# Normalizing attention rows after they are replicated, and letting the next chunk's first two score matmuls go ahead of the scaling of the last

## What is computed

```python
x = x + _L0_attn_ref(_layernorm(x), ...)     # the change is in here
x = x + _L0_ffn_ref(_layernorm(x), ...)      # shared MLP and 8 experts
x = x + _L1_attn_ref(_layernorm(x), ...)     # two scans (Mamba), forward and backward
x = x + _L1_ffn_ref(_layernorm(x), ...)      # int8-rounded matmul

# in _L0_attn_ref, 16 heads of 64, Qc and Rc of 128
scores = jnp.einsum('bqhd,bkhd->bhqk', Qc, Rc)
norm = jnp.sqrt(jnp.sum(jnp.square(scores), axis=-1, keepdims=True))
attn = scores / jnp.maximum(norm, NORM_EPS)            # NORM_EPS = 1e-12
out = jnp.einsum('bhqk,bkhd->bqhd', attn, Hv).reshape(B, S, D_MODEL)
return out @ Wo + bo
```

## Time and profile before

| | |
|---|---|
| median of 2 runs | 9504.41 us (9500.37 and 9508.46) |
| profiled execution, time | 9552.86 us |
| profiled execution, span of the slowest core (core 2) | 9551.2 us |
| spans of the 8 cores | 9483.5 to 9551.2 us |
| PE busy | 4446.2 us (47%) |
| DVE busy | 4802.7 us (50%) |
| ACT busy | 3157.2 us (33%) |
| mean granted TensorE clock | 0.61 |

### The profile page before, as it was taken

How to read it: one execution, slowest core, us unless ns; L and a number is a source line. 1 busy time by engine, 2 the same in 40 slices (tenths; PEclk the granted TensorE clock), 3 DMA queues, 4 the chain that set the end, 5 groups by cost and what they waited for, 6 DMA issues and landing times.

```text
span 9551.2 us, 57267 instructions; the slowest of 8 cores (9483.5 to 9551.2 us)
## 1 busy us (share of the span) xinstructions
PE 4446.2 (47%) x11136; PEld 1264.4 (13%) x11136; DVE 4802.7 (50%) x8041; ACT 3157.2 (33%) x4385; POOL 172.2 (2%) x221
## 2 busy tenths in 40 slices
PE   3644555455556499996323232333323232323334
PEld 1211111111111133111000000000000000000112
DVE  2334343344334321224467675757576776767445
ACT  3333323332332121002243443434252534444321
POOL 0000000000000100000000000000000000000000
PEclk8766766666666687666555555555555555555556
DMA  1042572100000133110000000000000000000000
GB/s 45 6 36 23 69 83 25 16 2 4 4 0 0 16 122 110 53 53 9 10 3 16 5 16 7 12 10 10 14 7 16 4 17 3 16 7 13 25 12 36
DMA packets 203005, 222.92 MB, mean 23 GB/s; under 512 B 131441, under 2 KB 140049, under 8 KB 200561
## 3 DMA queue, kind: packets, MB, share of 16 engines
q0 software_dynamic: 141104, 76.50, 7.3%
q1 hardware_dynamic: 61570, 142.76, 4.6%
HBM read 278.07 MB, written 65.03 MB: 36 GB/s over the span
## 4 chain that ended last, share of the span: by engine, by line
DVE 40%; PE 32%; issue 12%; ACT 12%; DMA 2%; DVEq 1%; POOL 0%; ACTq 0%; SPq 0%; POOLq 0%
DVE HBF L1721 14%; PE P2U L200 10%; PE PSU L200 6%; DVE DBXP L1717 5%; PE PSU L848 3%; PE PSU L857 3%; PE P3U L200 3%; DVE SROW L817 2%; DVE XCC L1446 2%; DVE SCBW L876 1%; DVEq L35 1%; PE P3U L1773 1%; DVE CARRY L1726 1%; PE P4U L200 1%; ACT L1645 1%
## 5 line engine op out<-in xcount | busy, mean ns | idle before, releaser
L1693 PE MATMUL P3U<-DBXP,EYEB 128*128 128x512 bf16 x1024 | 576.3, 563 | 1974.7 <-DVE DBXP L1728 1974.1
L1721 DVE TENSOR_TENSOR_SCAN HBF<-DAP,CARRY,DBXP 128x512 bf16<-128x512 bf16 x1024 | 1314.6, 1284 | 109.6 <-DVE DBXP L1717 4.1
L876 DVE CAST SCBW<-PSU 128x512 bf16<-128x512 f32 x512 | 354.1, 692 | 774.8 <-PE PSU L848 770.7
L1717 DVE TENSOR_TENSOR DBXP<-U_CH,BREP 128x512 bf16<-128x512 bf16 x1024 | 429.5, 419 | 309.2 <-ACT DAP L1645 187.3
L857 PE MATMUL PSU<-SCBW,HV 128*64 128x512 bf16 x960 | 465.1, 484 | 153.8 <-DVE SCBW L876 118.5
L848 PE MATMUL PSU<-QCB,RCB 128*128 128x512 bf16 x1024 | 477.7, 476 | 66.5 <-DVE ATTO L894 53.4
L886 ACT CAST SCBW<-PSU 128x512 bf16<-128x512 f32 x512 | 300.1, 586 | 570.4 <-PE PSU L848 569.7
L200 PE MATMUL P2U<-YLN,W1E 128*128 128x512 bf16 x512 | 462.1, 1079 | 10.6 <-DMA W1E<-wfsc 10.6
L1657 ACT ACTIVATE DAP<-DT_CH,ACOL 128x512 bf16<-128x512 bf16 x512 | 359.0, 719 | 304.1 <-DVE HBF L1721 298.8
L1693 PEld LDWEIGHTS P3U<-DBXP,EYEB 128*128 128x128 bf16 x1024 | 106.7, 104 | 2450.1 <-issue 2449.7
L1728 DVE TENSOR_TENSOR DBXP<-HBF,CREP 128x512 bf16<-128x512 bf16 x1024 | 424.9, 415 | 1.9 <-issue 1.9
(11 more groups left out here) (324 smaller groups left out, 7457.3 us busy)
## 6 DMA issues: line engine op xcount, KB each, us to landing
wfsc<-L_ffn_w POOLq DMA_DIRECT2D x16, 2048.0 KB, 90.4
SW1H<-wfsc SPq DMA_DIRECT2D x64, 256.0 KB, 2.7
SW3H<-wfsc SPq DMA_DIRECT2D x64, 256.0 KB, 2.9
SW2C<-wfsc SPq DMA_DIRECT2D x32, 512.0 KB, 4.0
W1E<-wfsc SPq DMA_DIRECT2D x8, 2048.0 KB, 12.2
W2E<-wfsc SPq DMA_DIRECT2D x8, 2048.0 KB, 7.8
WINS<-wmsc SPq DMA_DIRECT2D x64, 256.0 KB, 2.6
WINZ<-wmsc SPq DMA_DIRECT2D x64, 256.0 KB, 2.6
```

The source lines that it names most:

```text
L876: b.sV.inc(v.tensor_copy(SCBW[kt % 2][:], PSU[kt % 2][:, :]))
L1693: b.sT.inc(t.matmul(ybank[:, :], EYEB[:], DBXP[ni % 2][:], start=(ni == 0), stop=(ni == 7)))
L1717: b.sV.inc(v.tensor_mul(DBXP[ni % 2][:], U_CH[:, dt * QC:(dt + 1) * QC], BREP[:, ni * QC:(ni + 1) * QC]))
L1721: b.sV.inc(v.tensor_tensor_scan(HBF[ni % 2][:], DAP[ni % 4][:], DBXP[ni % 2][:], CARRY[:, dt * 16 + n: dt * 16 + n + 1], ALU.mult, ALU.add))
```

## The change

Two things are changed in the code of one head.

Steps 2 and 3 change places. The squared norms are replicated first (rn_mm, rn_ev), and square root, maximum and reciprocal are then taken on the replicated tile RNREP, on 128 partitions, in four pieces of 128x512, each in place: `_rne_s` (ScalarE) issues four square roots, `_rne_v` (VectorE) waits for each and issues its maximum and its reciprocal. The instructions on the 1x2048 row are gone (one square root, one maximum, one reciprocal), and twelve come in.

In `_sc_t`, scores 0 and 1 of chunks 1 to 3 of a head wait for the counts taken behind the copies of the chunk before (prev_sc), which don't contain L894. For chunk 0 they wait as before, now for `_rne_v` too. The wait for vcur, which contains L894 of the chunk before, now stands ahead of the values matmul of tile 0, the first to write PSU2.

```diff
--- before.py
+++ after.py
@@ -805,31 +805,38 @@
                         return s.copy(ROW_A[0:1, i * QC:(i + 1) * QC], bank[0:1, :])
                     mm_evac(NQ, ns_mm, ns_ev, [PSU[0], PSU[1]], "s")
 
-                    def _rn_s(s):
-                        b.sS.wait(s)
-                        b.sS.inc(s.activation(ROW_B, ROW_A, AF.Sqrt))
-                    b.s(_rn_s)
-
-                    def _rn_v(v):
-                        b.sS.wait(v)
-                        b.sV.inc(v.tensor_scalar(ROW_B, ROW_B, C_TINY[0:1, :], None, ALU.max))
-                        b.sV.wait(v)
-                        b.sV.inc(v.reciprocal(ROW_A, ROW_B))
-                    b.v(_rn_v)
-
                     def rn_mm(t, i, bank):
-                        if i == 0:
-                            b.sV.wait(t)
                         return mm_group(t, bank[:, :],
                                         [(ONESF[:], ROW_A[0:1, i * QC:(i + 1) * QC])])
 
                     def rn_ev(s, i, bank):
                         return s.copy(RNREP[:, i * QC:(i + 1) * QC], bank[:, :])
                     mm_evac(NQ, rn_mm, rn_ev, [PSU[0], PSU[1]], "s")
-
+                    sb_rn = b.sS.n
+
+                    def _rne_s(s):
+                        for qc in range(NQ):
+                            b.sS.wait(s)
+                            b.sS.inc(s.activation(RNREP[:, qc * QC:(qc + 1) * QC],
+                                                  RNREP[:, qc * QC:(qc + 1) * QC], AF.Sqrt))
+                    b.s(_rne_s)
+
+                    def _rne_v(v, sb_rn=sb_rn):
+                        for qc in range(NQ):
+                            b.sS.wait(v, sb_rn + qc + 1)
+                            b.sV.inc(v.tensor_scalar(RNREP[:, qc * QC:(qc + 1) * QC],
+                                                     RNREP[:, qc * QC:(qc + 1) * QC],
+                                                     C_TINY, None, ALU.max))
+                            b.sV.wait(v)
+                            b.sV.inc(v.reciprocal(RNREP[:, qc * QC:(qc + 1) * QC],
+                                                  RNREP[:, qc * QC:(qc + 1) * QC]))
+                    b.v(_rne_v)
+
+                    prev_sc = None
                     for qc in range(NQ):
                         scm, avm, evm2 = {}, {}, {}
                         vcur, scur = b.sV.n, b.sS.n
+                        kt2_v, kt2_s = prev_sc if prev_sc else (vcur, scur)
                         for kt in range(16):
                             if kt % 2 == 0:
                                 evm2[kt] = (b.sV, vcur + kt // 2 + 1)
@@ -837,11 +844,11 @@
                                 evm2[kt] = (b.sS, scur + kt // 2 + 1)
 
                         def _sc_t(t, qc=qc, scm=scm, avm=avm, evm2=evm2, vcur=vcur,
-                                  scur=scur, qcb=qcb, rcb=rcb, hh=hh):
+                                  kt2_v=kt2_v, kt2_s=kt2_s, qcb=qcb, rcb=rcb, hh=hh):
                             for kt in range(16):
                                 if kt < 2:
-                                    b.sV.wait(t, vcur)
-                                    b.sS.wait(t, scur)
+                                    b.sV.wait(t, kt2_v)
+                                    b.sS.wait(t, kt2_s)
                                 else:
                                     sm, cnt = evm2[kt - 2]
                                     sm.wait(t, cnt)
@@ -852,6 +859,8 @@
                                 scm[kt] = b.sT.n
                                 if kt >= 1:
                                     k2 = kt - 1
+                                    if k2 == 0:
+                                        b.sV.wait(t, vcur)
                                     sm, cnt = evm2[k2]
                                     sm.wait(t, cnt)
                                     b.sT.inc(t.matmul(
@@ -885,6 +894,7 @@
                                     b.sT.wait(s, avm[kt - 2])
                                 b.sS.inc(s.copy(SCBW[kt % 2][:], PSU[kt % 2][:, :]))
                         b.s(_sc_s)
+                        prev_sc = (b.sV.n, b.sS.n)
                         if hh == 1 and qc == NQ - 1:
                             pair_free[hp].append((b.sS, b.sS.n))
```

## The result

| | before | after |
|---|---|---|
| median, us | 9515.23 (10 runs, 9494.17 to 9564.32) | 9417.13 (11 runs, 9391.40 to 9457.40) |
| ratio | | 0.989, 95% interval 0.9869 to 0.9912 |
| span of the slowest core in the profile | 9551.2 (core 2) | 9439.9 (core 3) |
| mean granted clock of the cores | 0.611 to 0.618 | 0.620 to 0.626 |

The changed kernel is 1.1% faster; 9419 us with a range of 9370 to 9460 was predicted. The new instructions are the square root L820, maximum L827 and reciprocal L831, and the copy out of the replicated row is L813.

The account below looks back on a forecast made before the run. Bound: heads run serially on every engine, with the norms row alone and passages stalled by L894, ACT's branch and clock falls. Passages -56, clock -36, norms +7 make -85 us, from median 9504.4 to 9419; range 9370 to 9460.

Parts of the forecast that it names:

- The waits at a passage: Between chunks, scores 0 and 1 no longer wait for L894: 1.17 us sooner at 48 passages, 56 us saved.
- everything behind ACT comes 1.17 us sooner: At a passage, ACT's table load starts at 1084.47 instead of 1085.64, and all behind ACT moves with it.
- The clock: Behind passages, half of the 48 clock falls go, 36 us saved; bounds 0 to 72 us.
- price for a fall: Behind a passage, 12 matmuls at 0.55 instead of 0.43 us each: 1.5 us per clock fall.
- rival 1: The clock falls at every passage as before: -56 + 7, 9455 us; chance 0.18.
- The norms: From last L805 copy to first score, 18.65 us against 18.20: 0.45 us worse per head, +7 us over 16.
- the maximum: In the norms, each of four DVE maxima on 128x512 takes 0.49 us.
- the seven gaps: In the norms, seven gaps of 0.10 us between dependent DVE instructions, 0.70 us per head.
- The reciprocal itself: In the norms, each of four 128x512 reciprocals on DVE takes 3.35 us.
- rival 3: DVE's branch ends last at a passage: only 0.63 us won each, 30 us, giving 9481 us; chance 0.08.
- rival 4: In the norms, the wide reciprocal is dearer, 8.10 us each: 304 us more, 9723 us; chance 0.03.
- The wait for weights (WHD): Weight loads, 18.3 us once before; PE beginning to wait for them in each head would show the forecast wrong.

Follow-up runs that it names:

- x3_fill_before: Kernel before plus unread matmuls in chunks 1 to 3, three ahead of score 0 and one ahead of the first values matmul; 9430.84 us, ratio 0.9919.
- x8_all: Changed kernel plus ones-matrix norm sums, reciprocals in pieces behind VectorE's copies, three unread matmuls per passage and early table load; 8942.45 us, ratio 0.9402.

## Why the prediction was right, point by point

- **The waits at a passage: right in size, slightly high in worth.** 1.17 us sooner at the second values matmul was forecast; 4.20 to 3.02 was measured, 1.18. What a passage gained by it at a steady clock is 15.68 - 14.59 = 1.09 us: 52 us for 56. That everything behind ACT comes 1.17 us sooner is the step that is slightly wrong, since DVE takes over. In passages that keep their clock (x3_fill_before for the waits of before), DVE's first copy starts 1.97 us behind the last values matmul before and 1.22 after, and its third at 5.75 and 4.64. Its copies come 1.71 apart at the high clock; only the third of before is 0.36 later than that, because score 4 stands behind the values matmul that waits for ACT. So ACT's branch held the old passage up by 0.36 us beyond DVE's, and the changed one is decided by DVE, as the early table load confirms.
- **The clock: right in kind, and the half was luck.** The prediction took half of the falls as gone, from a new passage that lay between two that it could see; it says itself that no row decides it. 170 of 384 were left, 44%, so 56% were gone. It also has both stops ahead of the fall, but by the earlier trace rows the clock fell between 1085.9 and 1086.1, inside the second stop (1085.56 to 1086.27). Its price for a fall, 1.5 us, was 1.47 by the inserted matmuls, but a fall in the changed kernel costs 1.24, with 4.8 us at 0.50 in place of 6.9, so 45 us were won for the 36 forecast. The rule of the Trainium skill ("TensorE: Matmul & The Clock Gate", A second HAM failure mode: psum-queue depth-cycling), that small standstills between groups of matmuls make the clock swing, is borne out in what it says: 384 falls in 384 with the stops, 19 with matmuls in them, and swings go on with the one stop left. As a forecast of rival 1, falls at every passage, it did not hold, and a stop of 1.33 us with no fall behind it shows that a stop alone is not enough.
- **The norms: wrong in sign, by a small term.** +7 us was forecast and -7 measured. The steps that failed are the maximum and the seven gaps. The maximum was taken as 0.49 us four times, from the slope between 1024 and 2048 elements; the first took 0.49, those that follow another DVE instruction at once 0.39. The gaps were taken as 0.10 each; between a maximum and its own reciprocal it is that (1034.48 to 1034.58), but from a reciprocal to the next maximum, which does not depend on it, the next starts 0.08 before the recorded end (1034.17 and 1034.09). With 0.11 saved at the first replicating matmul that makes 0.3 + 0.54 + 0.11 = 0.95 us a head, and 0.45 less 0.95 is near the -0.48 seen. The reciprocal itself, forecast at 3.35 from the one on the row and two tiny ones, took 3.353.
- **The other rivals.** The DVE branch did not end last at the passage by the mark of the prediction (the second values matmul waits for ACT), yet at the high clock DVE decided the changed chunk as a whole: rival 3 had the right engine and, with 1.09 us in place of 0.63, not the price. It left out the 0.36 us by which ACT's branch was the later one before, and took 0.10 us for a gap that is 0.04 (1062.89 to 1062.93). A dear wide reciprocal (rival 4) is out. The wait for weights (WHD) did not grow: 14.2 us in all, for 18.3 before.
- **The sum.** By the traces -52 - 45 - 7 - 3 = -107 us, for -56 - 36 + 7 = -85. The clock's share was 9 us too small, the norms were 14 us off and the first chunks' 3 us not forecast; the waits were 4 us too large. The measured median stands 98 us below before's, between the two. That 9417 us lies within 2 us of the 9419 forecast is luck: the gain was 13 us larger than forecast, and before's median over more runs is 11 us above the one that the forecast started from.

## What to carry to other kernels

Price a wait by what the engine's clock does behind it as well as by its length: here stops of 1.11 and 0.71 us cost another 1.5. Whether that is so is cheaply tested by matmuls that nobody reads put into the stop; they leave all waits alone and show the clock's share by itself. Moving a serial piece of work from one partition to many gains nothing when its time goes by elements on the free side; hiding it in small pieces in idle time of its engine gained 209 us here (9199 to 8990), where the move gained 7 by the trace.

## What the runs showed of the hardware that was not expected

- In the kernel before, four matmuls a passage whose results are thrown away made the program 0.8% faster (0.9919, 0.9901 to 0.9937): the granted clock stayed at 1.00 over the passages, where it had fallen to 0.50 behind each.
- One unread matmul per passage did for the changed kernel nearly what three did: 10 falls and none, where 170 were without it.
- An independent DVE instruction behind a reciprocal starts 0.08 us before its recorded end, and a maximum of 128x512 takes 0.39 us there and 0.49 behind an idle stretch.
- A 128x512 reciprocal takes 3353 ns and a 128x64 one 543 ns, on 128 partitions; 1x2048 takes 12,941 ns.
- The granted clock has a level of 0.81 besides 1.00 and 0.50: on core 4 of x8_all the score matmuls take 437 ns in it and 389 at 1.00.
